# GNN block: three engines' operation order inside the first edge stage

## What is computed

```python
def _L0_gnn_ref(x, edge_index, W1, b1, W2, b2):
    row, col = (edge_index[0], edge_index[1])
    x_col = x[col]
    feat = jnp.concatenate([x_col, x[row] - x_col], axis=-1)
    h = jax.nn.relu(feat @ W1 + b1)
    messages = h @ W2 + b2
    out = jax.ops.segment_max(messages, col, num_segments=x.shape[0])
    out = jnp.where(jnp.isneginf(out), jnp.zeros_like(out), out)
    return out

def _L1_gnn_ref(x, edge_index, W1, b1, W2, b2, Wres, bres):
    src = edge_index[0]
    dst = edge_index[1]
    agg = jax.ops.segment_sum(x[src], dst, num_segments=x.shape[0])
    h = x + agg
    h = jnp.maximum(h @ W1 + b1, 0.0) @ W2 + b2
    res = x @ Wres + bres
    return res + h

edge_index = jnp.stack([src, dst])
x = _layernorm(x + _L0_gnn_ref(x, edge_index, ...), axis=-1)
x = _layernorm(x + _L1_gnn_ref(x, edge_index, ...), axis=-1)
```

## Time and profile before

| | |
|---|---|
| median of 3 runs | 1114.47 us (1114.39 to 1115.25) |
| the profiled execution's own time | 1113.68 us, its span 1111.9 us |
| TensorE busy (matmul) | 1068.9 us, 96% |
| VectorE, ScalarE, GpSimd busy | 934.9 us (84%), 896.9 us (81%), 765.8 us (69%) |
| granted TensorE clock, mean | 0.995 |
| chain that ended last, by engine | TensorE 65%, GpSimd 19%, issue 8%, VectorE 4%, ScalarE 2% |
| first edge stage | about 265 to 565 us of the span |

### The profile page before, as it was taken

One profiled execution on the slowest core, in us unless ns is written; L12 is line 12 of the kernel. 1 busy time (PEld: TensorE's weight loads), 2 busy tenths in 40 slices (PEclk: granted clock), 3 DMA queues, 4 the chain that ended last, 5 costly groups with the idle time before them and its releaser, 6 DMA issues.

```text
span 1111.9 us, 27074 instructions
## 1 busy us (share of the span) xinstructions
PE 1068.9 (96%) x7463; PEld 835.6 (75%) x7463; DVE 934.9 (84%) x3645; ACT 896.9 (81%) x3888; POOL 765.8 (69%) x798
## 2 busy tenths in 40 slices
PE   5899999999999999999899999999999999999995
PEld 3677877777666666666578888888888878888884
DVE  7799888897888888888868787878787789999993
ACT  2887878787888888888897888888888887777774
POOL 6777777777777777772047777777777777777712
PEclk9999999999999999999999999999999999999998
DMA  5788877875888888877576667676756566666652
GB/s 151 214 244 247 230 244 231 246 233 152 220 222 232 248 232 221 233 223 214 164 232 198 213 191 215 190 214 191 214 166 194 172 202 217 218 217 220 218 171 86
DMA packets 172255, 231.86 MB, mean 209 GB/s; under 512 B 25658, under 2 KB 90791, under 8 KB 172106
## 3 DMA queue, kind: packets, MB, share of 16 engines
q1 hardware_dynamic: 145434, 180.66, 52.0%
q0 software_dynamic: 25088, 48.94, 17.3%
q10 hardware_dynamic: 1584, 0.53, 0.2%
HBM read 129.48 MB, written 102.78 MB: 209 GB/s over the span
## 4 chain that ended last, share of the span: by engine, by line
PE 65%; POOL 19%; issue 8%; DVE 4%; ACT 2%; DMA 1%; SPq 0%; POOLq 0%; DVEq 0%; ACTq 0%
POOL edge_rows L522 17%; PE psY L1125 10%; PE psY L1126 10%; PE psH L1137 10%; PE psE L1118 6%; PE psT L1118 5%; PE psE L1257 4%; PE psE L1126 4%; PE psE L1125 4%; PE psE L1293 4%; PE psE L1248 3%; PE psE L1242 3%; PE psE L1240 3%; POOL xd_early L522 1%; DVE shared L758 1%
## 5 line engine op out<-in xcount | busy, mean ns | idle before, releaser
L1125 PE MATMUL psY<-wc,hT 128*128 128x128 f32 x1568 | 304.1, 276 | 0.5 <-DVE o_rows L646 0.4
L1126 PE MATMUL psY<-wcr,xT 128*128 128x128 f32 x1568 | 303.9, 276 | 0.0
L522 POOL DMA_INDIRECT edge_rows<-x1e_table,idx x196 | 188.8, 963 | 118.5 <-issue 59.4
L526 POOL DMA_INDIRECT out<-edge_rows,idx x196 | 195.0, 995 | 100.0 <-issue 61.9
L1125 PEld LDWEIGHTS psY<-wc,hT 128*128 128x128 f32 x1568 | 240.7, 192 | 13.3 <-issue 13.3
L949 ACT ACTIVATE junk<-psY 128x128 f32<-128x128 f32 x784 | 209.3, 302 | 49.3 <-PE psY L1126 49.1
L1126 PEld LDWEIGHTS psY<-wcr,xT 128*128 128x128 f32 x1568 | 238.8, 193 | 0.0
L522 POOL DMA_INDIRECT edge_rows<-in_x,idx x196 | 189.8, 968 | 65.5 <-issue 59.4
L609 DVE TENSOR_SCALAR x<-x_in,mv,rs 128x128 f32<-128x128 f32 x784 | 221.7, 361 | 0.6
L1137 PE MATMUL psH<-xT,wc 128*128 128x512 f32 x392 | 204.5, 604 | 6.2 <-ACT xT L944 5.5
L1118 PEld LDWEIGHTS psT<-ident,x 128*128 128x128 f32 x784 | 99.2, 143 | 110.1 <-issue 104.1
(11 more groups left out here) (125 smaller groups left out, 1993.4 us busy)
## 6 DMA issues: line engine op xcount, KB each, us to landing
x_in<-in_x SPq DMA_DIRECT2D x196, 256.0 KB
out<-o_rows SPq DMA_DIRECT2D x195, 256.0 KB
src_bc<-src_dram SPq DMA_DIRECT2D x49, 256.0 KB, 4.5
mask<-mask_dram SPq DMA_DIRECT2D x98, 128.0 KB
x1eT_spill<-x1eT SPq DMA_DIRECT2D x49, 256.0 KB, 2.4
x1e_table<-edge_rows SPq DMA_DIRECT2D x49, 256.0 KB, 3.5
x1e_table<-shared SPq DMA_DIRECT2D x49, 256.0 KB, 3.8
x1eT<-x1eT_spill SPq DMA_DIRECT2D x49, 256.0 KB, 3.1
```

The source lines that it names most:

```text
L522: nc.gpsimd.indirect_dma_start(to, None, table, bass.IndirectOffsetOnAxis(idx[:, what, t:t + 1], 0)).then_inc(landed[n % FLIGHT], 16)
L526: nc.gpsimd.indirect_dma_start(table, bass.IndirectOffsetOnAxis(idx[:, SCAT, t:t + 1], 0), frm, None, bounds_check=limit, oob_is_err=False ...
L1125: t_.matmul(to[:, cut(t)], h[:, cut(t)], wc2[:, :], start=t == 0, stop=False, skip_group_check=True)
L1126: last = t_.matmul(to[:, cut(t)], xt[:, cut(t)], wcr[:, :], start=False, stop=t == TILES - 1, skip_group_check=True)
```

## The change

Three engines' `step_a` are reordered, and the two waits on `psE1` follow the new order. No instruction is added or taken away.

```diff
@@ VectorE
             def step_a(s, n, h):
+                segment_max(s - 1)
+                residual0(s - 1)
                 both_recip(s)
                 scale_z(s)
-                segment_max(s - 1)
-                residual0(s - 1)
+                copy_xs(s + 1)
                 xs_stats(s)
                 xs_var(s)
-                copy_xs(s + 1)
@@ ScalarE
             def step_a(s, n, h):
+                relu0(s)
                 scale_xs(s)
-                relu0(s)
-                copy_x1eT(s - 2)
+                copy_xd(s + 1)
                 z_var(s - 1)
                 both_roots(s + 1)
-                copy_xd(s + 1)
+                copy_x1eT(s - 2)
@@ TensorE
                     wait(pe, xdT_done, g)
-                    wait(pe, x1eT_done, g - 2)
+                    wait(pe, x1eT_done, g - 3)
                     transpose4(psE[1], xd_rows(g), tx_done, dst_number(g))
...
                     pe.wait_ge(x1e_done, g + 1)
-                    pe.wait_ge(xdT_done, min(g + 3, GROUPS))
+                    pe.wait_ge(xdT_done, min(g + 4, GROUPS))
...
+                transpose_in(s + 1)
+                center_z(s - 1)
                 transpose_x1e(s - 2)
-                center_z(s - 1)
-                transpose_in(s + 1)
```

## The result

The changed kernel takes **1141.67 us** in the median of 5 runs (1138.4 to 1145.25) and the kernel before 1114.47 us in its runs beside it (1113.79 to 1115.25). The ratio is 1.0245, with a 95% interval of 1.0224 to 1.0266. The forecast was 1116.6 us with a range up to 1125.0, so the time lies far outside it, on the side of the mask rival. The profiled execution took 1145.25 us, 3.6 us above its median; its span is 1143.5 us against 1111.9.

What follows compares the result with a forecast made beforehand. TensorE was taken to set the pace in the first edge stage, with only its gaps to win. Cycles -1.0, LN transposes +0.8, start +1.8 and end +0.5 gave +2.1 us: 1116.6 us, range 1113.0 to 1125.0.

Steps and rivals of the forecast that it cites:

- mask rival: SyncE's mask load behind the later spill delays the scan: at 4.0 us 1124, at 4.5 near 1145; chance 0.18.
- The price per 0.1 us: Each 0.1 us of mask landing beyond the slack costs 0.1 x 43 steps = 4.3 us.
- The cycle without the mask: Four steps of the first edge stage take 23.3 to 23.5 us; -1 us over ten cycles.
- the centring's wait: Gap of 1.31 us in four steps, 0.99 at h = 1 where centring awaits VectorE's residual; all counted as removed.
- the relay: TensorE's transposes wait for `relu0` to read `psE0`: 0.95 us from product end, 1.22 us in four steps.
- LN transposes waiting for `copy_xd`: In each step LN transposes wait for `copy_xd`, both using `psE1`: +0.8 us, bounds 0 and 1.7.
- The relay being shorter: Rival: `relu0` and the weight preload overlap, so only h = 1 waits (0.5 us): 1109 us; chance 0.13.
- The start: Centring and LN transposes stand behind the wait for group 5's gathered rows; step 8 starts at 312.0: +1.8 us.
- The end: `copy_x1eT(47)` stands ahead of the dense unit on ScalarE, which feeds `scale_z`: +0.5 us, bounds 0 and 1.5.
- the `x` loads: At the end, loads of x behind SyncE's later spill may bite too; within bounds of 0 and 1.5 us.
- the `copy_xd` rival: If ScalarE is 0.2 us later, LN transposes wait in each of 43 steps: +8, 1124; chance 0.09.

Runs made afterwards that it cites:

- experiment 7: The changed kernel with SyncE's mask load behind the spill but ahead of the two stores: 1118.47 us, ratio 1.0043.
- experiment 1: The changed kernel with SyncE's mask load ahead of the spill and the two stores: 1118.84 us, ratio 1.0031.
- experiment 4: The changed kernel with the mask load first and the old order on all three engines in steps 0 to 5: 1115.43 us, ratio 1.0006.

## Why the prediction was wrong

- **The step that failed** is the mask rival's landing: "No row shows it ... So 3.1 to 4.5, and I take 3.6, nearest to its neighbour in the queue." It took 4.62 in the median, longer than both bounds, so a term that the sum had at nothing was worth some 23 us. The rest of that rival stands: the mask issued behind a spill that waits for the late `copy_x1eT`, and 3.8 us from which it decides (3.8 by the loop and by experiment 7). The choice between bounds that lay on both sides of the threshold was one for the chances, not for a value: 0.18 was far too little for a case which half of my own bracket (3.8 to 4.5) favoured. The bounds were also wrong as bounds: both neighbours are medians of another kind of transfer.
- **The price per 0.1 us was about twice too high**: I had each 0.1 us of lateness cost 0.1 in each of 43 steps. The loop runs over two steps, so by the loop it costs 0.05 in each. With the mean of 4.8 of the scans that a mask released, that is (4.8 - 3.8) / 2 = 0.5 us a step; 0.58 was measured (25.78 less 23.47, over four), of which the lower clock after the two latest masks can be 0.08 (3.4 us in 40 steps). The halving is worked out from the loop; no run varied the lateness alone. My rival's "at 4.5 near 1145" agreed with the result only because a landing too short met a price too high.
- **The cycle without the mask** was right: forecast 23.4, measured 23.47, the centring's wait gone and the relay in its place. `relu0` starts at 413.06 in experiment 1 and the transposes at 413.80, the same 0.74 us as in step 0 before.
- **LN transposes waiting for `copy_xd`**: forecast +0.8. Experiment 1 shows no such wait of TensorE between 310 and 545 us. The term was nothing.
- **The relay being shorter** did not come: 5.80 at h = 1 and not below.
- **The start**: forecast +1.8, measured +5.7 in the profile. The mechanism (centring and LN rows behind the wait for gathered rows) was right; left out were a second, earlier group (4) whose rows come late as well and the lower clock after those waits. It isn't the same in every run: the profile of experiment 1 has +0.4. In experiment 4 against 1 it was worth 3.4 us of the median.
- **The end**: forecast +0.5, about +3.3 in the profile from step 48 on (+31.6 less +28.35). Only 0.7 of it lies ahead of the centring of step 49, which stands behind a scan that waited 1.75 us. In experiment 1, where no mask is late, the same centring starts at 555.06 against 554.80. In the change it is this (TensorE's timeline), and with it the place behind it where most of the other 2.6 us went:

```profile
583.80 2.05 PE L1257 MATMUL psE<-center,shared 128*128 128x128 f32 x8 [3.41 <-DVE shared L748]
...
601.44 0.46 PE L1125 MATMUL psY<-wc,hT 128*128 128x128 f32 x2 [2.25 <-ACT o_rows L974]
```

  The dense `finish` (L974) had waited for VectorE's reciprocal, and that stood behind a wait of 3.68 us for a load of `x` (before: 1.56 us). The forecast had named the `x` loads in its bound for the end. Why this one came late isn't shown; experiment 1 has nothing of the 2.6 us.
- **A slip in the chances**: the list gives the `copy_xd` rival 0.09 and then 0.25 of it as slower; the 0.45 for slower comes out with 0.07.

With the mask term at its measured size, the forecast's other terms would have given 1116.6 plus 23, some 1140; the median is 1141.67. With the mask moved out of the way the forecast's 1116.6 lies at the top of the faster group of runs of experiment 1 and 2.2 us under its median of 1118.84.

## What to carry to other kernels

When a producer's step is moved later, follow every queue that waits for it to the last entry, and ask of each load behind that wait how much time is left until it is used; a load that does not depend on the wait belongs in front of it, and here one line moved in SyncE's queue was worth 23 us. If the margin lies within the bracket of an unmeasured landing, give that case its share of the chance rather than picking a value beside it, and work out over how many steps the loop closes before pricing the excess. And read a recurring gap for the piece that fills it: one dense piece cut in two won 5 us with no engine's order changed, where the reordering of three engines won none.

## What the runs showed of the hardware

- A 128 KB load of the mask from DRAM, issued by SyncE while the DMA engines were busy 0.71 of the time, let its waiting scan go after 3.9 to 5.5 us in 38 of 40 cases, median 4.62; in the kernel before, the store of twice the size ahead of it lands 3.8 us after its issue. Twice it took longer, and the cause is open (issue, wait and scan of the first; the other took 6.8):

```profile
377.40 1.28 DVE L758 TENSOR_TENSOR_SCAN shared<-mask,shared,psE 128x512 f32<-128x512 bf16 x1 [3.68 <-DMA mask<-mask_dram]
```

  Its mask had been issued at 369.39, 8.0 us before. The Trainium skill, page "DMA: Bandwidth & Descriptors", section "Anatomy of one DMA — SWDGE (gpsimd) path", gives about 2 us of fixed cost for a transfer on another path than SyncE's. An estimate of the mask's landing from that page's fit (2.0 us and the bytes over 436e3) is 2.3 us, half of what these rows show.
- That page's section "Queues, rings and completion order" says that a semaphore write follows all earlier writes of its DMA engine. The change's masks, none released earlier than 3.9 us from their issue, do not speak against it. With only the spill of their step ahead of them (experiment 7) two masks still took 4.97 and 4.89 us, and of the others the run gives only that they took no more than 4.8 to 5.2. What the 4.6 us are made of stays open.
- The granted clock fell to 0.71 over 283 to 291 us, after two waits of 1.42 and 1.99 us, and what followed ran slower (1.92 us for a centring that takes 1.13 at full clock). The product at 293.37 took 1.02 us again and the centring at 296.10 1.06. After a single wait of 2.23 us (458.95) the clock was 0.83 over 460 to 470 us, with two edge products of 1.91 and 1.88 us where 1.02 is usual.
